# A four-layer graph network on one core: layer 0's results taken ahead of layer 1's edges, and layer 1's output sum moved from VectorE to ScalarE and GpSimd

## What is computed

```python
x = _layernorm(x + L0(x, adj))   # softmax over rows of leaky_relu(s1_i + s2_j), times h
x = _layernorm(x + L1(x, adj))   # softmax over columns, times h, then elu
x = _layernorm(x + L2(x, adj))   # softmax over rows, times h, then elu; with biases
x = _layernorm(x + L3(x, adj))   # sum over r of (adj == r) @ x @ weight[r], plus bias
```

## Time and profile before

| | |
|---|---|
| median of 3 runs | 470.44 us (469.98 to 471.45) |
| profiled execution | 470.86 us, of which the span is 469.1 us |
| PE busy | 378.9 us, 81% |
| DVE busy | 375.9 us, 80% |
| ACT busy | 315.8 us, 67% |
| POOL busy | 290.5 us, 62% |
| granted TensorE clock, mean | 0.93 of 2.4 GHz |

### The profile page before, as it was taken

One profiled execution on the slowest core, in us unless ns is written; L12 is line 12 of the kernel. 1 busy time (PEld: TensorE's weight loads), 2 busy tenths in 40 slices (PEclk: granted clock), 3 DMA queues, 4 the chain that ended last, 5 costly groups with the idle time before them and its releaser, 6 DMA issues. The chain is left out here.

```text
span 469.1 us, 9311 instructions
## 1 busy us (share of the span) xinstructions
PE 378.9 (81%) x2818; PEld 337.8 (72%) x2825; DVE 375.9 (80%) x1414; ACT 315.8 (67%) x805; POOL 290.5 (62%) x425
## 2 busy tenths in 40 slices
PE   2789998998666779778697787899999959888870
PEld 2689998997666779678696676899999855455440
DVE  0167999999866899999999855598889997888862
ACT  1467999999534475565555655487778747787864
POOL 3236888887443545354453565478787886878882
PEclk9799999999777999899998899799999999999985
DMA  5998662000000000000000000000000000011122
GB/s 156 222 249 223 121 132 47 2 1 1 2 1 2 0 0 2 1 1 2 0 2 0 2 2 1 1 1 1 1 1 2 3 0 1 21 65 52 67 76 86
DMA packets 8757, 18.21 MB, mean 39 GB/s; under 512 B 1280, under 2 KB 2560, under 8 KB 8704
## 3 DMA queue, kind: packets, MB, share of 16 engines
q0 software_dynamic: 2304, 8.39, 9.4%
q1 hardware_dynamic: 2976, 4.52, 2.9%
q10 hardware_dynamic: 3424, 4.66, 2.8%
HBM read 21.76 MB, written 4.19 MB: 55 GB/s over the span
## 5 line engine op out<-in xcount | busy, mean ns | idle before, releaser
L461 PE MATMUL o_ps<-h_scaled,PT 128*128 128x129 f32 (+1 forms) x1536 | 193.8, 288 | 17.1 <-DVE y L953 14.2
L461 PEld LDWEIGHTS o_ps<-h_scaled,PT 128*128 128x128 f32 x1536 | 188.8, 204 | 18.5 <-issue 14.9
L669 ACT ACTIVATE X<-y,offset,rstd 128x128 f32<-128x128 f32 x256 | 104.9, 482 | 38.9 <-POOL offset L270 38.7
L901 DVE SCALAR_TENSOR_TENSOR PT<-rows_ps,factors,MT 128x512 f32<-128x512 f32 x128 | 88.8, 737 | 0.8 <-PE rows_ps L448 0.6
L403 PE MATMUL h_ps<-wx,xT 128*128 128x130 f32 x384 | 66.7, 314 | 27.9 <-DVE smax L856 26.9
L403 PEld LDWEIGHTS h_ps<-wx,xT 128*128 128x128 f32 x384 | 56.5, 211 | 38.3 <-issue 37.2
L261 POOL TENSOR_TENSOR rstd<-var_eps,neg_half 128x4 f32<-128x4 f32 x64 | 66.4, 1038 | 5.0
L973 DVE BATCH_NORM_STATS2 stats<-y 128x6 f32<-128x128 f32 x256 | 56.0, 281 | 7.0 <-DVE y L967 0.5
L276 POOL TENSOR_TENSOR elu_exp<-elu_exp,X 128x512 f32<-128x512 f32 x32 | 40.7, 1272 | 18.8 <-ACT elu_exp L663 18.5
L251 POOL TENSOR_TENSOR h_scaled<-hx,factors 128x516 f32<-128x516 f32 x32 | 33.6, 1050 | 24.7 <-PE o_ps L461 14.8
L227 POOL TENSOR_TENSOR mean_term<-h_mean,empty_row 128x512 f32<-128x512 f32 x32 | 38.2, 1192 | 16.9 <-DVE residual L953 15.3
(11 more groups left out here) (98 smaller groups left out, 664.6 us busy)
## 6 DMA issues: line engine op xcount, KB each, us to landing
MT<-adj_by_j POOLq DMA_DIRECT2D x16, 512.0 KB, 8.7
X<-x SPq DMA_DIRECT2D x16, 256.0 KB, 6.0
out<-X ACTq DMA_DIRECT2D x16, 256.0 KB, 2.0
w_rel<-w SPq DMA_DIRECT2D x1, 256.0 KB, 3.1
w_back<-w_by_output ACTq DMA_DIRECT2D x1, 192.0 KB, 3.1
wx<-w_by_input ACTq DMA_DIRECT2D x1, 192.0 KB, 5.9
bias<-b ACTq DMA_DIRECT2D x1, 64.0 KB, 4.5
bias<-b SPq DMA_DIRECT2D x1, 64.0 KB, 8.4
```

What stands on the lines that cost most here:

```text
L461: last = pe.matmul(o_ps[it.b][:, ic, first:1 + D], PT[:, it.b, jc, ic * P:(ic + 1) * P], h_scaled[:, it.b, jc, first:1 + D], start=(jc == ...
L669: last = act.activation(X[:, g, c, :], y[:, b, c, :], ACT.Identity, bias=offset[:, b, c:c + 1], scale=rstd[:, b, c:c + 1])
L901: dve.scalar_tensor_tensor(out=PT[:, it.b, c, :], in0=rows_ps[:], scalar=factors[:, it.b, 1, c:c + 1], in1=m, op0=ALU.max, op1=ALU.mult, * ...
```

## The change

- `take_out` of layer 0's items goes ahead of `edges` and of `node_terms` in VectorE's slot.
- The condition on `take_max` is now by item n alone: the maxima of the last two items before layer 2's steady slots are taken at the end of the slot before (slots 29 and 30), ahead of `finish`.
- Layer 1's y is no longer VectorE's. ScalarE writes elu_high = max(o, 0) from PSUM between the argument and exp; GpSimd adds elu_exp and elu_high behind `elu_low` (`add_high`). A new semaphore y_col counts these; `wait_y` picks it or y_sum by the item's layer. TensorE waits for elu_high in place of y where it writes layer 1's PSUM buffer anew.
- `split_bias2` goes to GpSimd, slot 24, with three copies by ScalarE in slot 26.
- The flag goes to layer 3's slots 54 to 58.

```diff
@@ gpsimd
+            def split_bias2():
+
+                pool.wait_ge(sem("b2_a"), 1)
+                pool.wait_ge(sem("b_in"), B_IN)
+                pool.tensor_tensor(bias2[:, D:D + 2], b2_a[:, :], ab2_sb[:, :], ALU.add).then_inc(sem("bias2"), 1)
...
+            def add_high(it):
+
+                pool.wait_ge(sem("elu_high"), it.of_layer)
+                pool.wait_ge(sem("x_new"), it.done - 2)
+                pool.wait_ge(sem("elu_low"), it.of_layer)
+                pool.tensor_tensor(y[:, it.b, :, :], elu_exp[:, :, :], elu_high[:, :, :], ALU.add)\
+                    .then_inc(sem("y_col"), 1)
+
             def attention_slot(at, n):
...
                 if at(-1) and at(-1).l == 1:
                     elu_low(at(-1))
+                    add_high(at(-1))
...
+                if n == G + 8:
+                    split_bias2()
@@ tensor, attend
-                if it.done > 2 and item(it.done - 3).l < 2:
-
-                    pe.wait_ge(sem("y_sum"), it.done - 2)
+                last = item(it.done - 3)
+                if last and last.l == 1:
+                    pe.wait_ge(sem("elu_high"), last.of_layer)
+                elif last and last.l == 0:
+                    wait_y(pe, last)
@@ tensor, attention_slot
-                if n == G + 2:
-
-                    pe.wait_ge(sem("flag_own"), 1)
-                    pe.wait_ge(sem("xT"), at(3).done)
-                    pe.transpose(xT_ps[:, 0:P], flag_own[:, 0:1].broadcast_to([P, P]), ident[:])\
-                        .then_inc(sem("flag_ps"), 1)
-                    pe.wait_ge(sem("flag_max"), 1)
-                    next_transpose(at(4))
@@ scalar, elu
                     act.activation(elu_low_arg[:, :, :], lin_ps, ACT.Relu, scale=-1.0)\
                         .then_inc(sem("elu_low_arg"), 1)
+                    if it.g >= 1:
+                        wait_y(act, item(it.done - 2))
+                    act.activation(elu_high[:, :, :], lin_ps, ACT.Relu).then_inc(sem("elu_high"), 1)
@@ scalar, attention_slot
+                if n == G + 10:
+
+                    act.wait_ge(sem("bias2"), 5)
+                    act.copy(bias2_parts[0:1, :], bias2_hi[0:1, :])
+                    act.copy(bias2_parts[32:33, :], bias2_mid[32:33, :])
+                    act.copy(bias2_parts[64:65, :], bias2_low[64:65, :]).then_inc(sem("bias2_parts"), 1)
@@ vector, attention_slot
             def attention_slot(at, n):
-                if n == 8:
-                    split_bias2()
                 if at(-1) and at(-1).l in (0, 2):
                     row_sums(at(-1))
-                if at(2) and not (at(2).l == 1 and at(0).l == 1):
+                if at(2) and not (at(0) and at(0).l == 1):
                     take_max(at(2))
                 if at(-1) and at(-1).l in (0, 2):
                     row_factors(at(-1))
+                if at(-2) and at(-2).l == 0:
+                    take_out(at(-2))
                 if at(1) and at(1).l == 1:
                     edges(at(1))
                 if at(2) and at(2).l == 1:
                     node_terms(at(2))
                 if at(3) and at(1) and at(1).l == 1:
                     own_max(at(3))
-                if at(-2) and at(-2).l == 0:
-                    take_out(at(-2))
...
-                if at(3) and at(3).l == 1 and at(1).l == 1:
+                if at(3) and at(1) and at(1).l == 1:
                     take_max(at(3))
                 if at(-1) and at(-1).l == 1:
-                    add_elu(at(-1))
                     finish(at(-1))
                     aggregate(at(-1))
-                if n == G + 1:
-
-                    dve.wait_ge(sem("flag_sum"), G)
...
@@ vector, relation_slot
+                if n == FLAG_SLOT:
+
+                    dve.wait_ge(sem("flag_sum"), G)
+                    dve.tensor_reduce(flag_own[:, 0:1], flag_sum[:, :, 0], AX.X, ALU.max).then_inc(sem("flag_own"), 1)
+                if n == FLAG_SLOT + 3:
+                    dve.wait_ge(sem("flag_ps"), 1)
+                    dve.tensor_reduce(flag_own[:, 1:2], smax_ps, AX.X, ALU.max).then_inc(sem("flag_max"), 1)
```

More of the change, by code:

```diff
@@ L158, in last_layers, with wait_y @@
             return slot
+        def wait_y(eng, it):
+            if it.l == 1:
+                eng.wait_ge(sem("y_col"), it.of_layer)
+            else:
+                eng.wait_ge(sem("y_sum"), it.done - (G if it.l > 0 else 0))
         def halves(it):
@@ L233, in add_residual @@
                 if it.g >= 2:
-                    pool.wait_ge(sem("y_sum"), it.done - 2)
+                    wait_y(pool, item(it.done - 3))
                 pool.wait_ge(sem(f"x_in{it.g}"), 16)
@@ L465, in attention_slot @@
             def attention_slot(at, n):
-                if at(4) and n != G + 2:
+                if at(4):
                     next_transpose(at(4))
@@ L511, in project_sum @@
                 else:
-                    pe.wait_ge(sem("y_sum"), it.done - 2)
+                    wait_y(pe, item(it.done - 3))
                 for c in range(C):
@@ L660, in elu @@
                 if it.done > G + 1:
-                    act.wait_ge(sem("y_sum"), it.done - 1)
+                    wait_y(act, item(it.done - 2))
                 act.wait_ge(sem("elu_low_arg"), it.done - G)
@@ L939, in take_out @@
                 if it.l == 2:
-                    dve.wait_ge(sem("y_sum"), it.done - 2)
+                    wait_y(dve, item(it.done - 3))
                 elif it.l > 0 or it.g >= 2:
@@ L965, in add_elu, with moments @@
                 dve.wait_ge(sem("x_new"), it.done - 2)
-                high = o_ps[it.b][:, :, 1:1 + D] if it.l == 1 else lin[:, it.b, :, :]
-                dve.scalar_tensor_tensor(out=y[:, it.b, :, :], in0=high, scalar=0.0,
+                dve.scalar_tensor_tensor(out=y[:, it.b, :, :], in0=lin[:, it.b, :, :], scalar=0.0,
                                          in1=elu_exp[:, :, :], op0=ALU.max, op1=ALU.add).then_inc(sem("y_sum"), 1)
-            def moments(b, y_sem, stats_sem, done):
-                dve.wait_ge(y_sem, done)
+            def moments(b, stats_sem):
                 for c in range(C):
@@ L986, in finish @@
                     dve.wait_ge(sem("mean_var"), it.done - 1)
-                moments(it.b, sem("y_sum"), sem("stats"), it.done)
+                wait_y(dve, it)
+                moments(it.b, sem("stats"))
             def aggregate(it):
@@ L1065, in relation_slot @@
                     aggregate(at(-1))
+                if n == FLAG_SLOT:
[4 more added lines that the diff above has]
+                    dve.tensor_reduce(flag_own[:, 1:2], smax_ps, AX.X, ALU.max).then_inc(sem("flag_max"), 1)
+                if n == FLAG_SLOT + 4:
+                    dve.wait_ge(sem("flag_max"), 1)
+                    dve.tensor_scalar(flag_int[:, :], flag_own[:, 1:2], 0.25 * C * N, None, ALU.is_gt)\
+                        .then_inc(sem("flag"), 1)
             def redo():
@@ L1180, in redo_moments @@
             def redo_moments(k):
-                moments(0, sem("re_y"), sem("re_stats"), k)
+                dve.wait_ge(sem("re_y"), k)
+                moments(0, sem("re_stats"))
                 mean_and_variance(0, sem("re_stats"), k, "re_mean_var")
```

38 lines of the change are left out of this document (17 added, 21 removed).

## The result

| | before | after |
|---|---|---|
| median | 470.94 us (469.98 to 472.20, 4 runs) | 482.01 us (478.79 to 486.57, 4 runs) |
| ratio after/before | | 1.0211 (95% interval 1.0141 to 1.0281) |
| profiled execution | 470.86 us, span 469.1 | 486.57 us, span 484.7 |

The change makes the kernel slower by 2.1%. The ratio leaves out one run of after, the profiled one, which is marked as a slow run (1.6% above the fastest of the four).

What follows compares the result with a forecast made beforehand. Bound: loops between engines, differing by layer; layer 1's steady slot VectorE's, a ScalarE-GpSimd loop close behind. Terms -9.8 + 0.2 - 1.4 + 1.6 + 19.7 + 3.0 = +13.3 on 470.86: 484.2, by median 483.8; range 466 to 490 us.

Steps and rivals of the forecast that it cites:

- The loop: Layer 1's steady slot: the ScalarE-GpSimd loop through the offset grows from 7.1 to 8.9 us by two new passes.
- The port waits: Layer 1's steady slot: GpSimd's rstd, neg_mean and offset wait for VectorE's weights passes, +1.2 us, making 10.1.
- rival D: Layer 1's slots: rstd holds the port for its whole 1.02 us, delaying a weights pass; 10.6 a slot, 489 us; chance 0.06.
- Slots 19 to 29: Layer 1's steady slots: 11 periods at 10.1 us instead of 8.31, +19.7 us; bias2's operations on GpSimd and ScalarE, +1.6.
- Layer 0: Slots before the seam: VectorE freed of bias2 in slot 8, -1.4 us; first edges of the seam about 1 us earlier.
- The seam: Layer 0 to 1, slots 15 to 18: layer 0's y ahead of edges ends the VectorE-TensorE mutual wait, -9.8 us.
- The flag late: Flag instructions moved from slots 17 and 18 to layer 3: +0.2 us there; the gain is counted at the seam.
- The end of layer 1: Slots 30 to 32: longer ScalarE-GpSimd loop and new passes, less VectorE's y, early maxima releasing nothing; together +3.0 us.
- rival C: Layer 1: TensorE becomes the bound, longer idles lowering its clock; about 10.6 us a slot, 489 us; chance 0.06.
- The two-sided case: Layer 1's slot length decides faster or slower: seam's gain and loop's loss are equal at about 9.15 us a slot.
- Rival A: Layer 1: the loop without port waits, 8.9 us a slot, seam at -12, in all 467.1 us; chance 0.15.

Runs made afterwards that it cites:

- e3: The changed kernel with layer 1's weights passes cut from 512 to 4 columns and the sum of weights held at 1 or more; 463.2 us, one run.
- e10: The changed kernel without ScalarE's new elu_high pass, so GpSimd adds a zero; 478.22 us, one run.
- e4: The changed kernel with GpSimd's find_rstd and find_offset ahead of elu_low and the addition in layer 1's slots; 460.74 us, ratio 0.9805.
- e11: The changed kernel with find_rstd and find_offset between elu_low and the addition on GpSimd; 452.31 us, one run.
- e2: The kernel before with only layer 1's y moved to ScalarE and GpSimd; 491.77 us, ratio 1.0476.
- e1: The changed kernel with layer 1's y left on VectorE as before, all else of the change kept; 454.67 us, ratio 0.9685.
- e5: The kernel before with only layer 0's take_out moved ahead of the edges; 458.97 us, ratio 0.9777.
- e6: The kernel before with only the flag moved late, to layer 3's slots; 469.72 us in ten runs, ratio 1.0008.
- e7: e1 with the condition on take_max as before, so the maxima at layer 1's end are late again; 456.01 us, ratio 0.9725.
- e9: e1 with find_rstd and find_offset ahead of elu_low on GpSimd in slots 31 and 32 only; 451.86 us, ratio 0.9638.

## Why the prediction was right

The forecast was 483.8 us; 482.01 was measured. Its mechanism is what the rows show, and the experiments took it apart. That the time came so close is in part luck: some terms were missed on either side, as told below. By its steps:

- **The loop** (7.1 + 0.34 + 1.44 = 8.9): right. e3 runs at 8.81, which is 7.1 + 0.27 + 1.44; the addition's 1.44 is in the rows (212.55 to 211.11), ScalarE's pass was 0.07 cheaper (e10).
- **The port waits** (0.5 + 0.4 + 0.3 = 1.2): right in sum and in each term: 0.50, 0.35, 0.33. The timeline worked out from r, the start of ScalarE's rows (208.46), holds too: node_terms began at r + 4.35, weights at r + 5.5 and not before.
- **Rstd as the exception** (rival D, 10.6 a slot): D is wrong. rstd runs from 214.06 to 215.59, and the pass of weights that begins at 214.65 takes 0.74. The Trainium skill (SBUF — State Buffer, section Who interferes with whom) has the exclusion last for the whole instruction. For the addition this case agrees (1.74 for a pass of weights in e4 and e11). For rstd it does not: of the 22 passes of weights in after that began while an rstd was under way, none took over 0.74.
- **Slots 19 to 29** (+19.7, and +1.6 for bias2 within them): 21.3 measured, 21.3 predicted, but by two errors that cancel. e2, which leaves bias2 where it was, takes 110.2 us, 10.02 a slot: +18.8, 0.9 less than forecast. The rest, 112.7 - 110.2 = 2.5 instead of 1.6, I put down to bias2, at the upper end of its bounds: after's slots are 10.01 up to slot 24 and longer from slot 25 on, and ScalarE's three copies put its rows back by 0.92 us, where the forecast had 0.4. It is dear only in after: in e1, where GpSimd isn't in the loop, the same split makes 0.4 (91.8 against 91.4).
- **Layer 0** (-1.4 for bias2, -1.0 for the earlier edges): -2.1 measured. e5, which has only layer 0's results first, has 1.2 of it, which leaves 1.0 for bias2.
- **The seam** (47.1 to 38.3): 39.2. Slots 15 to 17 came out as forecast, 8.7, 9.4 and 9.6 for 9.1, 9.0 and 9.8. Slot 18 was mis-sized: 11.5 for 10.4. The rows of after show what the step left out:

```profile
152.43 1.66 POOL L310 TENSOR_TENSOR y<-elu_exp,elu_high 128x512 f32<-128x512 f32 x1 [1.99 <-ACT X L707]
```

  The addition itself waits for layer 0's normalize, 1.99 us, and then meets the weights for another 0.4; the forecast had counted the addition between two normalizations, not what it waits for. The forecast's "-13 if no port wait meets it" was about right: e1's seam, 35.0, is 12.1 below before's, and its edges of slot 15 come 1.2 earlier by the order.
- **The flag late** (+0.2): not to be told from zero, as e6 shows. That 1.0 us of it stands bare at the seam, and comes back as time only once TensorE's wait for y is gone, the prediction did not say.
- **The end of layer 1** (+3.0): +2.7. Its parts are less sure than the sum. The early maxima "release nothing": with y on VectorE they bring about 1.0 us by the traces, too little for the timing. With the new order the move of y costs 5.4 (50.3 against e1's 44.9), with the old one 1.4 (e2's 49.0 against 47.6); the forecast had one price for both.
- **TensorE** (rival C): in layer 1's slots its mean granted clock fell from 0.91 to 0.83 of 2.4 GHz, the engine being busy for 62.57 us of 92 instead of 70.34; products of 3.74 us at the high level, 2.4 GHz (granted clock 1.00 from 180.1 to 183.8 us), alternate with some of 5.3 to 5.5 that spend a part at 1.2 GHz (0.69 from 191.0 to 196.3). But TensorE isn't late: ScalarE's rows follow normalize at once (208.46 after 206.82 + 1.65), and e4 and e11 change the slot without touching TensorE's queue. C's condition came in part, its price did not.
- **The two-sided case.** Rival A's slot (8.9) would have been right without the waits of 1.2 us; e3, which takes these away, has 8.81. Its slots 19 to 29 are 13.0 us shorter than after's, and taken from after's gap of 13.5 (the 15.6 of the spans less the later start) that leaves about nothing. So the waits decided between slower and the same, not between slower and A's 467.1. That A "decides at about 9.15 us a slot" goes with A's own terms (a seam of -12 gives 9.2); by the forecast's terms the balance lies at 8.31 + 6.4 / 11 = 8.9.

## What to carry over

Before work is moved from a busy engine to a less busy one, add up the loop that the work joins: GpSimd was idle for 38% of the time and still came to stand on the path that sets the slot, where 1.7 us of new passes and 1.2 us of waits cost more than the 0.8 us saved. Judge the parts of such a change apart, since here -16 us (e1 against before, from the first product on) and +29 us (after against e1) hid in one edit. The cheap gain lay in the order of one queue: put ahead what another engine waits for in the same slot, and do it only in those slots where the wait shows.

## What the hardware showed

- GpSimd's small operations (128 x 4) wait for a running VectorE pass of two SBUF operands: some 0.3 to 0.6 us each in layer 1, beside passes of 0.74. GpSimd's long one (128 x 512, 1.27 us) waits likewise (1.66 us at after's seam, 1.78 in e11), and then holds such a VectorE pass until it is over. What counts is how long GpSimd's runs, not VectorE's: in e3 a pass of weights over four columns began together with the addition and took 1.32 us, the next one 0.22.

```profile
206.81 1.32 DVE L923 SCALAR_TENSOR_TENSOR PT<-MT,empty_col,edge 128x4 f32<-128x4 bf16 x1
...
208.06 0.22 DVE L923 SCALAR_TENSOR_TENSOR PT<-MT,empty_col,edge 128x4 f32<-128x4 bf16 x1
```

- rstd, a power of 128 x 4 values that takes 1.02 us, held no pass of weights: those beside it keep their 0.74 (22 in after).
- The same code starts at different times. The first product of layer 0 began between 26.2 and 30.9 us in the kernels profiled; e1 and e7, which are the same up to the end of layer 1, began it at 26.2 and 29.5. Whether this makes up the spread of one kernel's timings (e1: 451.72 to 458.65, 6.9 us) is not shown, since each kernel has one profile. Stretches between marked instructions can be compared to some tenths of a microsecond (the seam of e1, e7 and e9: 35.0, 35.0 and 34.7) where whole times can't.
